# First diffusion step: logits of a pair's second tile taken in three places of the first half round

## The reference, cut to what matters

```python
def _top_p_attention(X, W1, W2, W3):
    q = X @ W1.T @ W2.T
    k = X @ W3.T
    logits = q @ k.T / TAU
    probs = jax.nn.softmax(logits, axis=-1)
    ...                     # sort, cumulative sum, keep until 0.9 is reached
    A = probs * mask
    return A / jnp.maximum(A.sum(-1, keepdims=True), 1e-12)
for n in range(STEPS):      # STEPS = 2
    A = _top_p_attention(Xa, W1, W2, W3)
    Xf = R @ Xf             # R: the row-normalised adjacency with the identity
    Xa = A @ Xa
    Z = Z + Xf @ U1[n].T + Xa @ U2[n].T
```

## Time and profile before

| | us |
|---|---|
| median of 3 runs | 3041.66 (3039.34 to 3041.97) |
| the profiled execution, its own time | 3042.38 |
| its span, first to last instruction | 3040.7 |
| busy: TensorE, VectorE, ScalarE, GpSimd | 2323.6, 1941.9, 1232.8, 638.9 |
| mean granted clock of TensorE | 0.893 |

### The profile page before, as it was taken

How to read it: one execution, slowest core, us unless ns; L and a number is a source line. 1 busy time by engine, 2 the same in 40 slices (tenths; PEclk the granted TensorE clock), 3 DMA queues, 4 the chain that set the end, 5 groups by cost and what they waited for, 6 DMA issues and landing times. The chain is left out here.

```text
span 3040.7 us, 44231 instructions
## 1 busy us (share of the span) xinstructions
PE 2323.6 (76%) x14310; PEld 1704.2 (56%) x14310; DVE 1941.9 (64%) x4668; ACT 1232.8 (41%) x1981; POOL 638.9 (21%) x1649
## 2 busy tenths in 40 slices
PE   4499999498728999869825873877555499999999
PEld 3377777286406778758504752766444244444468
DVE  5567777433247786784338788888873577777741
ACT  3466555212356666642366763766412100000000
POOL 2000000200134443430044542545302200000000
PEclk9699999799759999989857987999777699999999
DMA  1322221063100000000100000000004000000012
GB/s 45 117 96 95 95 95 57 13 205 112 41 17 13 27 19 23 18 22 18 43 17 6 16 15 6 16 11 15 10 10 152 1 1 0 0 0 0 0 49 94
DMA packets 49299, 120.85 MB, mean 40 GB/s; under 512 B 5952, under 2 KB 24672, under 8 KB 45792
## 3 DMA queue, kind: packets, MB, share of 16 engines
q1 hardware_dynamic: 49120, 118.83, 11.3%
HBM read 93.85 MB, written 24.97 MB: 39 GB/s over the span
## 5 line engine op out<-in xcount | busy, mean ns | idle before, releaser
L1892 DVE SCALAR_TENSOR_TENSOR fil_acc<-bank,fil_node,fil_acc 128x256 f32<-128x256 f32 x682 | 330.0, 484 | 110.0 <-PE bank L1960 97.4
L1346 PE MATMUL bank<-idf,X 128*128 128x128 f32 x968 | 138.6, 306 | 205.3 <-DVE step_recips L1810 205.3
L1423 ACT ACTIVATE step_PT<-bank 128x512 f32<-128x512 f32 (+1 forms) x264 | 128.1, 575 | 371.1 <-PE bank L1346 371.1
L1958 PE MATMUL bank<-parts_in,fil_xTh 128*128 128x512 f16 x704 | 268.4, 381 | 0.0
L1959 PE MATMUL bank<-parts_in,fil_xTh 128*128 128x512 f16 x704 | 268.3, 381 | 0.0
L1960 PE MATMUL bank<-parts_in,fil_xTl 128*128 128x512 f16 x704 | 268.1, 381 | 0.0
L1356 PE MATMUL bank<-kH,qHL 128*128 128x512 f16 (+1 forms) x264 | 105.9, 401 | 195.0 <-ACT step_E L1432 150.4
L1346 PEld LDWEIGHTS bank<-idf,X 128*128 128x128 f32 x968 | 122.3, 157 | 217.4 <-DVE step_recips L1810 208.6
L722 PE MATMUL bank<-V,HL 128*128 128x256 f32 x968 | 236.0, 386 | 0.2
L1378 PE MATMUL bank<-H,step_PT 128*128 128x256 f32 x968 | 216.0, 379 | 0.0
L1378 PE MATMUL bank<-A,step_PT 128*128 128x256 f32 x968 | 216.0, 379 | 0.0
(11 more groups left out here) (382 smaller groups left out, 5056.7 us busy)
## 6 DMA issues: line engine op xcount, KB each, us to landing
gat_A<-in_adj SPq DMA_DIRECT2D x22, 1408.0 KB, 5.9
step_a<-adjT SPq DMA_DIRECT2D x44, 352.0 KB, 2.9
gcn_raw<-in_L_W SPq DMA_DIRECT2D x16, 512.0 KB, 4.8
split<-gcn_halves SPq DMA_DIRECT2D x16, 512.0 KB, 3.4
parts_in<-split SPq DMA_DIRECT2D x4, 2048.0 KB, 19.3
adjT<-gat_a SPq DMA_DIRECT2D x22, 352.0 KB, 2.3
gcn_a<-adjT SPq DMA_DIRECT2D x22, 352.0 KB, 4.0
out_a<-adjT SPq DMA_DIRECT2D x22, 352.0 KB, 2.9
```

Of the source, the lines that this page charges most:

```text
L1346: last = pe.transpose(p_bank[n % nb][:, i * 128:i * 128 + 128], M[j][:, (b + i) * 128:(b + i) * 128 + 128], core.idf[:])
L1423: act.activation(PT[:, b * 128:(b + m) * 128], p_bank[n % len(p_bank)][:, 0:m * 128], ACT.Copy).then_inc(pT_done, 1)
L1892: c(dve.scalar_tensor_tensor(out=acc[k][:], in0=ps, scalar=node[k][:, n:n + 1], in1=acc[k][:], op0=ALU.mult, op1=ALU.add))
L1958: pe.matmul(w_bank[n % 4][:], xTh[k][:, x], wh[:, blk], start=c == 0, stop=False)
```

## The change

In the first diffusion step (`evals == 1`) the logits of tile 1 move ahead in the round. On TensorE chunks 0 and 1 come before the first half of attend of tile 0, chunks 2 and 3 before its second half, chunks 4 and 5 after it; the three parts of neighbours of tile 1 then follow in one piece. On ScalarE the copies of chunks 0 and 1 come between tile 0's exponentials and its Relu pass, those of chunks 2 to 5 between its Relu pass and its Sign pass. No instruction is added or taken away, and the second step's order stays.

```diff
+            def pair_spread():
+                rows = [[(2, lambda p, q, j=j, n=n: neighbours(p, j, n)) for n in range(3)] for j in range(2)]
+                chunks = [[(0, lambda p, q, j=j, n=n: logits(p, q, j, n)) for n in range(NL)] for j in range(2)]
+                return [*chunks[0][0:2], rows[0][0], *chunks[0][2:4], rows[0][1], *chunks[0][4:], rows[0][2],
+                        (2, lambda p, q: all_transposes(p, 0)), (3, lambda p, q: turn(p, 1)), *chunks[1][0:2],
+                        (2, lambda p, q: attend(p, 0, 0)), (3, lambda p, q: mix(p, 1)), *chunks[1][2:4],
+                        (2, lambda p, q: attend(p, 0, 1)), *chunks[1][4:], *rows[1],
+                        (2, lambda p, q: all_transposes(p, 1)), (2, lambda p, q: turn(p, 0)),
+                        (2, lambda p, q: attend(p, 1, 0)), (2, lambda p, q: mix(p, 0)),
+                        (2, lambda p, q: attend(p, 1, 1))]
-            in_order(pe, [*half(0, 3), *half(1, 2)], T // 2)
+            in_order(pe, pair_spread() if evals == 1 else [*half(0, 3), *half(1, 2)], T // 2)
...
-            def first_sums(p, q, j):
+            def first_relu(p, q, j):        # exp of the chance, then the Relu pass
...
+            def first_sign(p, q, j):        # the Sign pass, then the bell
...
+                chunks = [(0, lambda p, q, n=n: evacuate(p, q, 1, n)) for n in range(NL)]
-                in_order(act, [logits_0, turned_0, products_1, exponentials_0, first_0,
-                                logits_1, turned_1, products_0, exponentials_1, first_1], T // 2)
+                in_order(act, [logits_0, turned_0, products_1, exponentials_0, *chunks[0:2],
+                                (0, lambda p, q: first_relu(p, q, 0)), *chunks[2:],
+                                (0, lambda p, q: first_sign(p, q, 0)),
+                                turned_1, products_0, exponentials_1, first_1], T // 2)
```

More of the change, by code:

```diff
@@ L1445, in exponentials, with sums @@
                 act.activation(at(mass, q, j), at(mass, q, j), ACT.Exp, scale=-1.0).then_inc(exp_done, 1)
-            def sums(p, q, j, r, S):
+            def sums(p, q, j, r, S, which=(0, 1)):
                 t = p * 2 + j
-                for i, (func, a) in enumerate(((ACT.Relu, under), (ACT.Sign, signs))):
+                for i in which:
+                    func, a = ((ACT.Relu, under), (ACT.Sign, signs))[i]
                     n = 2 * r + i
@@ L1462, in first_sums @@
                 core.fence(act)
-                sums(p, q, j, 0, first)
+                sums(p, q, j, 0, first, (0,))
+            def first_sign(p, q, j):
+                t = p * 2 + j
+                sums(p, q, j, 0, first, (1,))
                 act.wait_ge(guessed, t * 2 + 2)
@@ L1466, in first_sums @@
                                scale=0.5 / QUANTILE ** 2).then_inc(begun, 1)
+            def first_sums(p, q, j):
+                first_relu(p, q, j)
+                first_sign(p, q, j)
             def second_sums(p, q, j):
```

## The result

The changed kernel took 3046.27 us (median of 20 runs, 3041.33 to 3049.74), the kernel before, on the same chip, 3041.55 (20 runs, 3035.96 to 3044.57): ratio 1.0017, 95% interval 1.0010 to 1.0024. It is slower by about 0.17%, inside what I had called no change, but it moved the other way than forecast (3037.8) and lies above my range (3033 to 3045). The profiled execution took 3046.53, with a span of 3044.8 against 3040.7.

A forecast was written before the change was run, and what follows sets the result against it. No engine is full; a ring of waits through all bounds the round. First rounds gain 1.6, six steady rounds lose 2.6, round 8 gains 3.7, the last 1.4: 4.1, taken as 3.9 off 3041.66, giving 3037.8; range 3033 to 3045.

The forecast's parts named there:

- TensorE's clock: TensorE's one gathered wait per steady round, before tile 0's chunk 2: some 2.4, under the 2.88 after which the clock held.
- Rival (b): TensorE's clock falls in the gathered wait of every round, 3.4 a time, seven times 24: about 3062; chance 0.06.
- the ring: Steady round's path through ScalarE's first copies, TensorE's tile 0, `take_0`, sort, `keep_0`, `largest_1`, exponentials 1: 45.98 a round.
- The first rounds: Rounds 0 and 1, without a take and bound by ScalarE's own order: round 2 starts 2.4 earlier.
- GpSimd's block: Round 0: VectorE's `below_0` blocks GpSimd for 3.03, delaying `guess_1`; gain 0.95, up to 3.4 without that overlap.
- Rival (a): TensorE's clock falls only in round 8's gap of 3.7 between mix and chunk 2: 3.4 given back, 3041.2; chance 0.20.
- Rival (c): Faster: `take_0` does not bound the round, VectorE's 43.9 does; about 3028; chance 0.08.
- Rival (d): GpSimd's `newton_0` runs late before `guess_1`, a round loses up to 1: 3041 to 3045; chance 0.06.
- Rival (e): The moved copies change nothing visible, each round keeping its length by another near-equal way: 3041.7; chance 0.05.

The follow-up runs named there:

- the first experiment: Ten needless 512-column matmuls added to the changed kernel, in TensorE's wait before tile 0's chunk 2 from round 3 on: 3040.23 us, ratio 0.9997.

## Why the prediction was wrong

**The step that failed** is the one headed TensorE's clock: "2.4 lies under the gap that held". It took one held clock, after 2.88, as a length below which the clock holds. The clock fell in this wait, or just behind it, in all of rounds 3 to 8 and 10. The wait was also taken 0.3 to 0.6 too short, 2.4 where 2.67 to 3.06 was measured, but that is not what failed: with three needless matmuls the clock fell at 2.17 to 2.41, and with TensorE's order alone it held at 2.77. Rival (b) had the mechanism and the place, with a chance of 0.06. The price was wrong the other way: 3.4 a fall, where the traces show 1.6, since the slow stretch here covers only four logits matmuls and 14 of neighbours. The 3.4 had been read from the mean clock of round 8 of before, one long gap in one round; for a fall in round 8's gap the first experiment does give 3.2. (The 0.60 in rows 9 is two short matmuls in one row, not one to set beside 0.39; at full clock the same row takes 0.45, in the kernel with ScalarE's order alone, so the reading of a slow clock was right.) By the forecast's own terms with 1.6 in six places on the ring (rounds 3 to 7 and 10; round 8's is covered) it is 9.6 less 4.1, 5.5 slower, where the step measured 5.2.

**The price of the even rounds.** The rest of the ring was right: 46.10 where the clock held, 46.0 forecast (the sum, 21.86 and 11.72, is 33.58 and not 33.61; that changes nothing); 46.2 with the wait filled; the waits of 2 before exponentials 1, of 5 before `take_0`, of none before `finish_0`; 49.27 for round 8, 49.6 forecast.

**The first rounds**: 2.35 gained by round 2's start, 2.4 forecast, and GpSimd's block is there. The bound for round 0 without the block, a gain of up to 3.4, was too low: with `guess_1` first the round is 35.37, 4.9 less than before, so the block was worth 3.7 and not 2.4.

**Rival (a)** did not occur in this kernel: its gap was 1.41, not 3.7, as mix ended at L+17.5 instead of L+15.8 after the fall at the round's start, and chunk 2 started at L+18.9 instead of 19.5 with VectorE's smaller delay (6.46 for 6.85). It occurred in the first experiment, where that fall is absent, with nearly the price given, and again, after a wait of 4.12, in the kernel with the second third of neighbours moved. **Rival (c)** is out: attend does wait behind the chunks, and with both delays taken out the round goes to 44.2, near VectorE's 43.9. **Rival (d)** is out, since no steady round shows it: in round 4 `newton_0` ends at L+33.4, later than the L+32.2 given, but `guess_1` starts only 2.2 after that. **Rival (e)** is out: the rounds changed, all of them.

**What should have been seen.** The rule of the Trainium skill that I named ("TensorE: Matmul & The Clock Gate", Part 1) spoke against gathering waits, and the traces of the changed kernel agree: seven waits of 2.67 to 3.06, seven falls. The kernel with TensorE's order alone, with waits of 2.67 to 3.03 at the same place, has one fall in eight, so the rule would not have told the two kernels apart. I set one held clock after 2.88 against it. That row was one occurrence, in another stretch of work, and could not carry so much. Besides, the rival's size had been written as a sum over seven falls at once, 24; with 1.6 to 3.4 each, a range that reaches to slower would have followed from the same rows.

**What stays open**: what makes the clock fall in one wait and not in another. It is not the wait's length alone. Held: 2.00 (round 9), 2.03 (three needless matmuls, round 3), 2.67 to 2.84 (TensorE's order alone), 2.88 (before, round 6), 3.65 (ScalarE's order alone, round 8). Fell: 2.17 to 2.41 (three needless matmuls, rounds 4 to 8 and 10), 2.67 to 3.06 (here), 3.03 (TensorE's order alone, round 7), 3.24 and 4.12 to 5.05 (round 8 of several). At 2.77 both occur, with the same instructions directly before and behind the wait, so what decides lies elsewhere, and no run here varied that by itself. One thing shows: in the changed kernel the slow stretches of rounds 3 to 8 begin 47.79 apart (968.16, 1015.95, 1063.74, 1111.52, 1159.31, 1207.10), although the rounds are 47.49 to 47.90 long and the stretch slides from 0.5 before the wait's end to just behind it.

## What to carry to other kernels

An order that moves an engine's work to where it waited anyway also gathers what was left of its waits elsewhere: list TensorE's waits before and after, longest first, and where several small ones become one of 2 to 3 us in each round, as here, allow for a fall of the clock in every one and price it by the work that follows directly on the path; the same wait fell in seven rounds of seven in one kernel and in one of eight in another, so the length alone does not settle it. Then fill that wait with work that is due anyway; here a move of one line within the list turned +0.17% into -0.4%, and a second one into -0.6%. Try each engine's half of a reordering by itself: here ScalarE's half alone was worth -0.2%, and TensorE's half took it back.

## What was not expected of the hardware

A fall of the clock does not have one price. At the round's start it was 1.6 (slow for some 3 of work: four matmuls 0.43 apart, then 14 in 2.26), in round 8 of the first experiment 3.2 (attend 7.07 for 4.91). And it need not coincide with the wait: with three needless matmuls the first three matmuls behind a wait of 2.17 still ran at 2.4 GHz, and the slow ones began 0.7 after it ended. And a wait of 2.77 at one and the same place was followed by a slow clock in one kernel and by a full one in another. Adding 2.3 of matmuls without use to every round from round 3 on shortened rounds 3 to 7 by 1.3 to 1.6.
